# More result buffers, earlier token scatters and a filler before each indirect DMA in a routed feed-forward layer

## The reference

```python
def _L0_ffn_ref(x, gate_w, expert_gate, expert_up, expert_down, shared_gate, shared_up, shared_down):
    TOP_K = 2
    def _ffn(x, gw, uw, dw):
        return jax.nn.silu(x @ gw.T) * (x @ uw.T) @ dw.T
    xf = x.reshape(-1, H)
    shared = _ffn(xf, shared_gate, shared_up, shared_down)
    logits = xf @ gate_w.T
    probs = jax.nn.softmax(logits, axis=-1)
    topw, topi = jax.lax.top_k(probs, TOP_K)
    topw = topw / (topw.sum(-1, keepdims=True) + 1e-20)
    comb = jnp.zeros((T, E), xf.dtype).at[jnp.arange(T)[:, None], topi].add(topw)
    def body(acc, ws):
        gw, uw, dw, wcol = ws
        return (acc + _ffn(xf, gw, uw, dw) * wcol[:, None], None)
    routed, _ = jax.lax.scan(body, jnp.zeros_like(xf), (expert_gate, expert_up, expert_down, comb.T))
    return (shared + routed).reshape(B, S, H)
x = _layernorm(x + _L0_attn_ref(x, ...), axis=-1)
x = _layernorm(x + _L0_ffn_ref(x, ...), axis=-1)
```

## Time and profile before

| | |
|---|---|
| median of 3 runs | 1244.45 us |
| the profiled execution: span from first to last instruction | 1288.1 us |
| time around that span in the profiled execution | not given by the profile |
| PE busy | 1067.3 us, 83% |
| PE weight loads busy | 725.3 us, 56% |
| DVE busy | 829.4 us, 64% |
| ACT busy | 695.8 us, 54% |
| POOL busy | 703.8 us, 55% |
| mean granted TensorE clock | 0.941 |

### The profile page before, as it was taken

How to read it: one execution, slowest core, us unless ns; L and a number is a source line. 1 busy time by engine, 2 the same in 40 slices (tenths; PEclk the granted TensorE clock), 3 DMA queues, 4 the chain that set the end, 5 groups by cost and what they waited for, 6 DMA issues and landing times. The chain is left out here.

```text
span 1288.1 us, 28760 instructions
## 1 busy us (share of the span) xinstructions
PE 1067.3 (83%) x9396; PEld 725.3 (56%) x9396; DVE 829.4 (64%) x2134; ACT 695.8 (54%) x1513; POOL 703.8 (55%) x1166
## 2 busy tenths in 40 slices
PE   1677898898989988999888849988878879999990
PEld 0333444444444443444444328877777779999880
DVE  2667888898888988988887137732222226655594
ACT  1016666666666664766667714454444446666430
POOL 0004554454545543777677722655555537888686
PEclk9958999999999998999999858999999889999995
DMA  5624534344344442553341224222222123333242
GB/s 93 75 40 68 82 65 77 79 70 82 68 77 84 69 77 46 88 109 88 75 107 27 69 62 171 60 60 61 62 60 59 52 56 104 113 108 106 76 120 73
DMA packets 124769, 100.48 MB, mean 78 GB/s; under 512 B 19952, under 2 KB 115574, under 8 KB 124178
## 3 DMA queue, kind: packets, MB, share of 16 engines
q1 hardware_dynamic: 114786, 76.55, 29.6%
q0 software_dynamic: 8704, 16.87, 4.1%
q10 hardware_dynamic: 1136, 5.23, 1.2%
HBM read 37.88 MB, written 35.79 MB: 57 GB/s over the span
## 5 line engine op out<-in xcount | busy, mean ns | idle before, releaser
L709 ACT ACTIVATE probs<-scores 128x512 f32<-128x512 f32 x640 | 346.7, 599 | 112.5 <-PE scores L622 105.4
L772 POOL TENSOR_SCALAR_AFFINE_SELECT probs<-probs 128x256 f32<-128x256 f32 (+1 forms) x640 | 234.5, 380 | 248.6 <-ACT probs L709 238.5
L599 PE MATMUL maxed<-kstack,qstack 52*128 52x128 bf16 (+3 forms) x1152 | 223.2, 299 | 71.0 <-DMA kstack<-parts 38.3
L622 PE MATMUL scores<-qstack,kstack 64*128 64x512 bf16 (+3 forms) x1024 | 236.1, 304 | 40.9 <-ACT probs L709 17.4
L1145 DVE TENSOR_TENSOR e_hid<-e_gate,e_up_ps 128x352 f32<-128x352 f32 (+2 forms) x192 | 107.6, 561 | 234.5 <-ACT e_gate L1368 149.1
L919 DVE TENSOR_REDUCE maxA<-maxed 128x4 f32<-128x512 f32 x256 | 165.6, 684 | 81.1 <-PE maxed L606 80.4
L1432 POOL DMA_INDIRECT y_tokens<-e_raw,e_row_i x144 | 145.6, 1011 | 120.2 <-ACT e_raw L1393 81.2
L638 PE MATMUL pv<-probs,vaug 128*32 128x512 f32 (+3 forms) x2048 | 197.7, 460 | 2.9 <-POOL probs L772 2.9
L919 DVE TENSOR_REDUCE maxB<-maxed 128x4 f32<-128x512 f32 x256 | 162.4, 682 | 4.9 <-PE maxed L606 4.9
L604 PE MATMUL maxed<-causal,halves 64*128 64x256 bf16 (+1 forms) x640 | 159.7, 261 | 0.0
L622 PEld LDWEIGHTS scores<-qstack,kstack 64*128 64x128 bf16 x1024 | 75.7, 94 | 145.8 <-ACT probs L709 81.5
(11 more groups left out here) (160 smaller groups left out, 1824.1 us busy)
## 6 DMA issues: line engine op xcount, KB each, us to landing
qstack<-parts SPq DMA_DIRECT2D x192, 64.0 KB
kstack<-parts SPq DMA_DIRECT2D x192, 64.0 KB
x_sorted<-zeros SPq DMA_DIRECT2D x16, 580.5 KB
e_xs<-x_sorted SPq DMA_DIRECT2D x144, 64.5 KB
e_raw<-y_tokens SPq DMA_DIRECT2D x64, 128.0 KB
xin<-in_x SPq DMA_DIRECT2D x16, 256.0 KB, 3.1
xres<-in_x SPq DMA_DIRECT2D x16, 256.0 KB
x1T_all<-ynT SPq DMA_DIRECT2D x16, 256.0 KB
```

Of the source, the lines that this page charges most:

```text
L599: pe.matmul(bank[:, at:at + (k1 - k0) * P], q[rows, slot, i * P:(i + 1) * P], ks[rows, slot, k0 * P:k1 * P], start=first, stop=False, skip ...
L622: last = pe.matmul(scores[st.at(0, SEQ_UNITS, n) % SB][:, col:col + width], ks[rows, slot, kt * P:(kt + 1) * P], q[rows, slot, kt * P:T], ...
L709: act.activation(probs[g % 2][:, u * T:(u + 1) * T], scores[st.at(0, SEQ_UNITS, UNITS * g + u) % SB][:], ACT.Exp).then_inc(S["exp_done"], 1)
L772: pool.affine_select(out=view, in_=view, compare_op=ALU.is_ge, fill=0.0, base=0, pattern=pattern, channel_multiplier=-1).then_inc(S["maske ...
```

## The change

1. `YTURN = 24`: the results go into 24 `ys` buffers in turn. ACT waits for the scatter of the result 24 before it. There are 24 semaphores for the landings, and both halves share them.
2. Scatters of the second half's tokens: in steps 10 to 23 POOL issues one per step and a second one in every odd step, 21 in all. The other 43 come one behind each of results 0 to 42.
3. Filler: `take_pause()`, a memset of 128x256 f32 on POOL, stands ahead of each of the 64 token scatters and of each of the 144 result scatters, 208 in all. It waits only for the filler before it.
4. `MIX`: the first half's tile t is mixed in step 116 + floor(8t/5), so five tiles in eight steps from step 116 to step 165; its first load is in step 112. The second half's mixing stays as it was.

```diff
-MIX = ((PARTED + CSLOT + 4, 2), (PARTED + NSLOT + 5, 1))
+MIX = ((PARTED + CSLOT + 20, 8, 5), (PARTED + NSLOT + 5, 1, 1))
 SPLIT_AT = 8
-PACE = 7
+PAUSE = 256
+YTURN = 24
...
-    for chunk, (first, every) in enumerate(MIX):
-        turn, rest = divmod(step - first, every)
-        if rest == 0 and 0 <= turn - lag < CT:
-            return chunk * CT + turn - lag
+    for chunk, (first, steps, turns) in enumerate(MIX):
+        for t in range(CT):
+            if first + (t + lag) * steps // turns == step:
+                return chunk * CT + t
...
                         if t == 0:
-                            for slot in range(TURN):
-                                sp.wait_ge(y_stored[chunk][slot], STORED)
+                            for slot in range(YTURN):
+                                sp.wait_ge(y_stored[slot], STORED * (chunk + 1))
...
-                        chunk, tile = divmod(n, CSLOT)
-                        slot = n % TURN
+                        slot = n % YTURN
                         act.wait_ge(S["y_ready"], n + 1)
-                        if tile >= TURN:
-                            act.wait_ge(y_stored[chunk][slot], 16 * (tile // TURN))
-                        elif chunk:
-                            act.wait_ge(y_stored[0][slot], STORED)
+                        if n >= YTURN:
+                            act.wait_ge(y_stored[slot], 16 * (n // YTURN))
...
+                def take_pause():
+
+                    if pauses[0]:
+                        pool.wait_ge(S["paused"], pauses[0])
+                    pool.memset(pause[:], 0.0).then_inc(S["paused"], 1)
+                    pauses[0] += 1
...
+                    take_pause()
                     scatter(pool, keep, dram, 1, t, choice, S["x_scattered"])
...
-                        if step % 4 == 3:
+                        if step % 2:
                             scatter_next()
                     kind, n = tile_at(step + DOWN)
                     if kind == ROUTED:
-                        chunk, slot = n // CSLOT, n % TURN
+                        chunk, slot = n // CSLOT, n % YTURN
+                        take_pause()
                         pool.wait_ge(S["y_taken"], n + 1)
...
-                                                oob_is_err=False).then_inc(y_stored[chunk][slot], 16)
-                        if chunk == 0 and (n + 1) * PACE // 10 > n * PACE // 10:
-                            scatter_next()
+                                                oob_is_err=False).then_inc(y_stored[slot], 16)
+                        scatter_next()
```

More of the change, by code:

```diff
@@ L1031, in experts @@
         hT = [sb(f"hT{n}", [P, NCH * P]) for n in range(2)]
[L1033 to L1037, removed]
+        after_raw = raw[:].rearrange("p e w f -> p (e w f)")[:, 0:(YTURN + 4 * TURN) * C].rearrange("p (n c) -> p n c", c=C)
+        ys = after_raw[:, 0:YTURN]
+        picked = after_raw[:, YTURN:YTURN + 2 * TURN].rearrange("p (s n) c -> p s n c", n=2)
+        mixed = after_raw[:, YTURN + 2 * TURN:YTURN + 3 * TURN]
+        result = after_raw[:, YTURN + 3 * TURN:YTURN + 4 * TURN]
         stats = sb("stats", [P, TURN, 6])
@@ L1042, in experts @@
         rstd = sb("rstd", [P, TURN])
+        pause = sb("pause", [P, PAUSE])
         gate_ps = [ps(f"gate_ps{n}") for n in range(2)]
@@ L1052, in experts @@
             silu_done hid_done h_ready hT_kept y_ready y_taken half_set mix_half mixed stats_taken aggregated stats_ready
-            rstd_ready result_ready group_kept group_rest group_ready group_taken""".split()
+            rstd_ready result_ready paused group_kept group_rest group_ready group_taken""".split()
         S = {n: sem(n) for n in names}
@@ L1056, in experts @@
         xs_loaded = [sem(f"xs_loaded{n}") for n in range(TURN)]
-        y_stored = [[sem(f"y{c}_stored{n}") for n in range(TURN)] for c in range(CHUNKS)]
+        y_stored = [sem(f"y_stored{n}") for n in range(YTURN)]
         picked_in = [sem(f"picked_in{n}") for n in range(TURN)]
@@ L1060, in experts @@
         CONSTS, EXPERTS_IN = 16 * 2, 16 * 4
-        STORED = 16 * (CSLOT // TURN)
+        STORED = 16 * (CSLOT // YTURN)
         def split_at(step):
@@ L1398, in _ @@
                 pool.wait_ge(S["half_set"], 1)
-                scattered = [0]
+                scattered, pauses = [0], [0]
+                def take_pause():
[3 more added lines that the diff above has]
+                    pauses[0] += 1
                 def scatter_next():
```

## The result

| | before | changed |
|---|---|---|
| timed median | 1244.20 us (1239.36 to 1244.94, 4 runs) | 1263.16 us (1257.02 to 1269.34, 4 runs) |
| ratio, with its 95% interval | | 1.0157 (1.0114 to 1.0200) |
| profiled execution, span | 1288.1 us | 1255.3 us |

The changed kernel is slower by 1.6%, 19 us. I had forecast 1221, faster; the nearest of my cases was the rival of 1268. The span fell by 32.8 us while the timed median rose by 19, which is the sign that I had given for that rival.

The account below looks back on a forecast made before the run. PE's late news was taken to bound the first half; with fillers POOL would bind, its 329.5 us from 844.6 putting step 168 at 1174.1 instead of 1199.13. So 1244.45 - 24 = 1220.5, forecast 1221 us, range 1203 to 1269.

Parts of the forecast that it names:

- the sign that I had given for that rival: Whole program: a profiled span shorter by some 24 us with a timed median that is not would show rival (1).
- if this difference lies elsewhere and stays: Whole program: the profiled span's 43.65 us above the timed median stays, so 1244.45 - 24 = 1220.5 us timed.
- the late news: First half: ACT copies results later behind PE's first matmul than the usual 0.87 us; blamed on dense runs of indirect DMAs.
- The 54 us: First half: 0.83 us more per result than PE's 2.09, over 65 results; fillers were to remove it from PE's account.
- rival (1): First half: late news only in the profiled execution, fillers still cost; 1268 us (1254 to 1281), chance 0.26, by half 0.10.
- PE's news is on time again: First half: with fillers, scatters 1.53 us apart instead of 1.27 to 1.29 no longer delay PE's news; 54 us gone.
- Rival (2): First half: the filler doesn't end the late news; 43 x 0.74 = 32 us more, 1252 us; chance 0.15.
- POOL as the bound of everything up to step 168: First result to PE's step 168: POOL's 329.5 us end at 1174.1; PE alone would be there at 1137.
- The shared steps: Before the first result: fillers delay the remainder that PE needs from POOL, 4 us together (2 to 6).
- The wait at the half's end: PE's wait at 1036.97 for rows, SP held by the last token scatter: goes, or shrinks to under 4 us.
- The mixing: Second half: five tiles in eight steps plus each result's scatter take POOL 2.52 us per step, over PE's 2.09.
- The 6.7 us: Shared steps: by the shared-port rule 21 fillers could hold DVE up to 21 x 0.32 = 6.7 us; sum 1221 to 1228.

## Why the prediction was wrong

**The step that failed: "if this difference lies elsewhere and stays".** I took the 43.65 us between the profiled span and the timed median for something outside the change's reach. It was the late news itself: by their marks, the profile came from a slow chip and the times from a fast one. The 54 us that the filler was to give back were never lost in the timed runs. The same text held the right arithmetic under rival (1): 2.18 us per result instead of 2.92, "48 us less, nearly the whole difference". I gave it 0.26 (and 0.10 to half of it), on the ground that nothing showed tracing to delay PE. That was true, and beside the point: a run on a slow chip has the late news in its timed median too, and a profile on a fast chip has none. I asked only what tracing does, not whether the two executions ran under the same conditions. That 1263 lies within my range of 1203 to 1269 is no merit of the forecast, whose own range was 1206 to 1237: the rest was there for the rivals.

**The filler's cure: wrong too.** "PE's news is on time again" rested on one run of three DMAs at 1.53 and 1.63. On a slow chip 34 of 72 copies are late with fillers, 33 without. The first half does get shorter there by 20 us (209.9 to 189.9), and the kernel without fillers has 201.7: of the 54 us the fillers brought some 12 (across two chips), or 9 in the kernel before, and behind result 71 POOL's longer account took them back. Rival (2) was right on its mechanism for slow chips: the ratio is 1.0060, slower. At 1.69 the news is on time, in one trace: so the step may have failed in size and not in kind. I took 1.53 for far enough from 1.29 because three DMAs in a row showed no delay, a run too short to tell. So the forecast would have failed on either kind of chip.

**On a fast chip, point by point.** POOL as the bound of everything up to step 168: yes; 1163.5 instead of 1174.1, of which 182 x (1.53 - 1.48) = 9.1 is the filler's period. Rival (1) put the timed kernel before at step 168 at "about 1151" with result 0 at 839.5 to 840.6, that is some 311 behind it; measured 1160.3 - 849.7 = 310.6, counted from PE's start of result 0. Its +24 was 16.7, mostly the filler's period again. The shared steps: 4 us forecast, 2.2 measured. The 24 buffers: enough at 1.48 (copies never late), as forecast; not at 1.69. The wait at the half's end: gone, as forecast. The mixing: 2.52 per step forecast, 2.45 measured. One sign came out wrong: PE was to have no wait of over 2 us for a tile's rows, and it has one of 5.85 and one of 2.33. I had let POOL's pace reach PE through DVE, which may be only four tiles ahead; I had left out that SP waits for POOL ahead of each store and keeps the rows back meanwhile.

**The fillers and DVE.** The 6.7 us that I had drawn from the Trainium skill, "SBUF — State Buffer", section "Who interferes with whom", as what the fillers might cost DVE were not seen: in the shared steps DVE's 28 products e_hid take 657 ns in the mean with the fillers, 655 without. They were drawn too simply. For a DVE instruction with two inputs in SBUF the section names only GpSimd instructions that read SBUF, and a memset only writes. The traces agree: of the 16 DVE instructions of L1080, which have two such inputs, the 7 that run beside a memset and a DMA take 0.51 us in the mean, and the two beside POOL instructions that read SBUF, its remainder e_group_x among them, take 1.30 and 1.33. Which DVE instruction meets that remainder is a matter of place. With fillers (DVE, then POOL), and then without:

```profile
823.94 2.00 DVE L1109 TENSOR_SCALAR e_norm<-e_norm 128x64 f32<-128x64 f32 x1
824.35 1.29 POOL L1427 TENSOR_TENSOR e_group_x<-e_group_in,e_group_x 128x512 fp32r<-128x512 f32 x1
825.57 0.32 POOL L1404 MEMSET e_pause<- 128x256 f32 x1
```

```profile
829.99 1.87 DVE L1080 TENSOR_TENSOR e_w_in<-e_raw,e_w_in 128x352 fp32r<-128x352 f32 x1
830.17 1.30 POOL L1424 TENSOR_TENSOR e_group_x<-e_group_in,e_group_x 128x512 fp32r<-128x512 f32 x1
```

Without fillers the instruction of the second fence waits, and L1109 behind it takes 0.18 us; with them it takes 0.53, and L1109 takes 2.00. So the 16 instructions of L1080 take 615 ns in the mean with the fillers and 750 without, 2.2 us less in all, and L1109 takes 1.8 us more. L1109 ends 0.05 us behind the memset and 0.30 behind the remainder, so the memset may have held it too, for 0.3 us at the most; nothing here tells the two apart.

## What to carry to other kernels

Before a stall in a profile is priced, compare the profiled execution's own time with the timed runs. Where they differ by 44 us, ask first whether the stall that you mean to remove is the difference, and take a profile again beside timed runs on the same chip. A change that adds work to an engine with little room (25 us here over 72 results) has to be summed on that engine for both cases, with the stall and without. Ask also which queue the busy engine's output stands in: here SP's wait for POOL's last multiply kept PE's rows back. And split a bundle: here the 24 buffers and the earlier token scatters alone gain 0.9% on a fast chip, the later mixing takes that back but for 0.15%, and the fillers turn it into a loss of 1.6%.

## What the runs showed of the hardware

The same kernel takes 1246 to 1250 us on some chips and 1293 to 1295 on others, with a mean granted clock of 0.93 to 0.94 on both, and 49.3 of 50 us of the difference lie in the first half, where POOL issues indirect DMAs back to back: on slow chips ACT's copies start 3.0 to 4.0 us behind the matmuls at the places shown, on fast chips 0.87. On a slow chip 33 to 44 of 72 copies are late at 1.29 us between scatters and 34 to 40 at 1.48; at 1.69, in one trace, 8 are, results 61 to 68, where the 24 buffers have run out. Why the chips differ stays open, and so does whether it is the chip or the time: no run here tells it. A memset of 256 columns between indirect DMAs adds 0.20 us to their period (1.28 to 1.48), not its 0.33, since the wait ahead of the DMA falls from 0.30 to 0.16.
